# Two expert stages rewritten: 64 experts taken in pairs with matmul parts side by side, 8 experts' results written apart, deeper rings

## The reference

```
# layers 0, 2 (and a shared expert beside them); CAPACITY 160
h = einsum('ech,efh->ecf', buf, expert_w1)         # buf: 64 x 160 x 128
x1, x2 = split(h, 2, axis=-1)                      # 384 columns each
out = einsum('ecf,ehf->ech', x1 * silu(x2), expert_w2)
combined = zeros((T, H)).at[st].add(y)             # y = out * its gate
# layers 9, 11; capacity 1280
h = gelu(einsum('ecd,edf->ecf', padded_x, w1))     # 8 x 1280 x 128, 256 columns
out_w = out_rep * w_topk;  result = out_w.reshape(T, 2, D).sum(axis=1)
```

## Time and profile before

| | us |
|---|---|
| median of 3 runs (lowest, highest) | 4105.83 (4065.69, 4126.18) |
| the profiled execution | 4105.43 |
| its span, first to last instruction | 4103.7 |
| stretch of l0f1e, l0f2e | 262, 272 |
| stretch of l3f1e, l3f2e | 167, 164 |
| stretch of l2a, l3f1a, l3f2a | 404, 359, 367 |

### The profile page before, as it was taken

One profiled execution on the slowest core, in us unless ns is written; L12 is line 12 of the kernel. 1 busy time (PEld: TensorE's weight loads), 2 busy tenths in 40 slices (PEclk: granted clock), 3 DMA queues, 4 the chain that ended last, 5 costly groups with the idle time before them and its releaser, 6 DMA issues. The chain is left out here.

```text
span 4103.7 us, 70296 instructions
## 1 busy us (share of the span) xinstructions
PE 2727.5 (66%) x24900; PEld 1763.1 (43%) x24900; DVE 2230.5 (54%) x5930; ACT 1408.5 (34%) x2942; POOL 2017.8 (49%) x2409
## 2 busy tenths in 40 slices
PE   3348837544885546599966997361688876998361
PEld 1238824322774233355544554350233333554351
DVE  6743357567223524577734774214599995774313
ACT  1112213221111314156531664122666750664121
POOL 4757730174565302167731112686678772111685
...
GB/s 307 40 42 216 209 85 34 28 61 4 185 199 172 206 144 30 9 16 17 14 6 16 18 19 12 94 130 57 83 71 54 82 42 14 19 19 5 74 149 81
...
## 3 DMA queue, kind: packets, MB, share of 16 engines
...
...
## 5 line engine op out<-in xcount | busy, mean ns | idle before, releaser
L3256 PE MATMUL l3am_y<-l3am_hc,ident 128*128 128x512 f32 x512 | 285.6, 642 | 92.8 <-DVE l3am_hc L3165 92.7
L2945 POOL TENSOR_TENSOR l3am_db<-l3am_du,l3am_bs 128x512 f32<-128x512 f32 x256 | 317.8, 1271 | 43.9 <-DVE l3am_hh L3157 43.9
L3157 DVE TENSOR_TENSOR_SCAN l3am_hh<-l3am_dA,l3am_db 128x512 f32<-128x512 f32 x256 | 300.9, 1210 | 49.5 <-ACT l3am_dA L3065 48.3
L768 POOL TENSOR_TENSOR l2a_pT<-l2a_pT,l2a_kept 128x512 int32<-128x512 int32 x192 | 241.7, 1273 | 136.5 <-ACT l2a_pT L979 135.8
L2355 POOL DMA_INDIRECT l0f_table<-l0f2e_y,l0f2e_idx x128 | 178.8, 1397 | 133.6 <-DVE l0f2e_idx L2335 66.2
L869 DVE CUSTOM_DVE_ANT_0 l2a_junk<-l2a_s,l2a_addend 128x256 f32<-128x256 f32 x512 | 187.4, 421 | 83.0 <-PE l2a_s L1093 69.4
L2355 POOL DMA_INDIRECT l0f_table<-l0f1e_y,l0f1e_idx x128 | 178.8, 1397 | 80.7 <-issue 32.6
L2002 POOL DMA_INDIRECT l0f_rows<-l0f1r_row,l0f1r_idx x160 | 174.0, 1087 | 89.4 <-issue 86.6
L862 DVE TENSOR_REDUCE l3f2a_mx<-l3f2a_s 128x2 f32<-128x512 f32 x256 | 165.6, 686 | 67.2 <-PE l3f2a_s L1093 66.0
L862 DVE TENSOR_REDUCE l3f1a_mx<-l3f1a_s 128x2 f32<-128x512 f32 x256 | 165.6, 686 | 67.1 <-PE l3f1a_s L1093 65.8
L3256 PEld LDWEIGHTS l3am_y<-l3am_hc,ident 128*128 128x128 f32 x512 | 93.2, 198 | 227.1 <-DVE l3am_hc L3165 173.1
...
## 6 DMA issues: line engine op xcount, KB each, us to landing
...
l3f_rows<-blank SPq DMA_DIRECT2D x8, 1370.0 KB, 10.4
```

The lines of the kernel that those rows point to most:

```text
L768: self.nc.gpsimd.tensor_tensor(t, t, self.kept[:, f // 8 % 2, :].unsqueeze(1).to_broadcast([P, 2, 2 * P]), ALU.mult).then_inc(self.cut_g, 1)
L2945: G.tensor_tensor(db[j][n % 2][:, :], du[j][k % 2][:, :], bs[s // QUARTER][:, s % QUARTER, :], ALU.mult).then_inc(db_ready[j], 1)
L3157: V.tensor_tensor_scan(hh[j][n % 2][:, :], dA[j][n % 2][:, :], db[j][n % 2][:, :], 0.0, ALU.mult, ALU.add).then_inc(h_ready, 1)
L3256: T.matmul(yb[j][:, :], c.ident[:, :], hc[j][n % 2][:, :], start=(s == 0), stop=(s == N - 1)).then_inc(summed, 1)
```

## The change

1. **64 experts** (`paired_experts`): a unit is two experts, 320 slots, in pieces of 128, 128 and 64 rows; 32 units. `h` has one pair of banks for each expert q of the pair, used again by the next pair. In `output` the middle piece holds 32 rows of the first expert and 32 + 64 of the second, as three matmuls placed at columns 0, 32 and 64 of the array. DVE makes y with five operations. POOL issues three adds for a pair, each with waits for adds of the pair before; piece 0 goes to table 0, pieces 1 (but for its 32 first rows) and 2 to table 1. y is four deep.
2. **Matrices** (`Matrices`): a ring of 8 experts' matrices, the first 8 loaded during `route`. For 8 experts that is all of them.
3. **8 experts** (`experts`): a token's first choice goes to table 0, its second to table 1, by a number that `route` puts in the row, so the transfer writes and doesn't add; y and indices are five deep. A row is 144 numbers for 137; an empty slot's number is out of bounds and is skipped.
4. **Attentions**: strip 0 is filled by DVE, the others by POOL after `va`; `l3f1a` and `l3f2a` begin with the statistics before the weights are waited for; the mask of `l2a` is built in `l1at` (the last phase of `l1a`), its 16-fold compare and reduce replaced by 16 operations on 256 elements; in `l2a` ACT's normalisation moves from u = 1 to u = 4, behind the queries and keys.

The diff, cut to what is spoken of:

```diff
+            nc.vector.memset(c.blank[8][:, :, D + 8:], FAR).then_inc(blank_made, 1)
...
+    def strips(self, eng, n, made):
+        eng.memset(self.qk[n][:, :, 0, :], 0.0).then_inc(made, 1)
+        eng.memset(self.qk[n][:, :, 1, :], 1.0).then_inc(made, 1)
     def pool_setup(self, g):
         nc = self.nc
-        nc.gpsimd.memset(self.none[:, :], 0.0).then_inc(self.made, 1)
-        for t in self.qk:
-            nc.gpsimd.memset(t[:, :, 0, :], 0.0).then_inc(self.made, 1)
-            nc.gpsimd.memset(t[:, :, 1, :], 1.0).then_inc(self.made, 1)
...
+        for n in range(1, 4):
+            self.strips(nc.gpsimd, n, self.made)
+    def dve_setup(self):
+        self.nc.vector.memset(self.none[:, :], 0.0).then_inc(self.first_made, 1)
+        self.strips(self.nc.vector, 0, self.first_made)
...
-    def dve(self, v, finish, more=None):
+    def dve(self, v, finish, more=None, early=None):
         self.dve_stats(v, 0)
+        self.dve_setup()
+        if early:
+            early()
...
-            if u == 1 and self.real(b + 4) and self.kept is not None:
-                self.act_normal(a, b + 4)
...
+            if u == (1 if b == -4 else 4) and self.real(b + 4) and self.kept is not None:
+                self.act_normal(a, b + 4)
...
+        link(nc.vector.tensor_scalar(hit_k, cpos, gf[:, 0:1], None, ALU.is_equal))
+        for n in range(1, self.NG):
+            link(nc.vector.scalar_tensor_tensor(hit_k, cpos, gf[:, n:n + 1], hit_k, ALU.is_equal, ALU.max))
...
-                link(nc.vector.tensor_tensor(hit[:, :, :], cpos[:, :].unsqueeze(1).to_broadcast([P, NG, SEQ]),
-                                             gf[:, :].unsqueeze(2).to_broadcast([P, NG, SEQ]), ALU.is_equal))
-                link(nc.vector.tensor_reduce(hit_k[:, :], hit[:, :, :].rearrange("p g s -> p s g"), AX_X, ALU.max))
...
-        self.E, self.R = E, D + E + 1
+        self.E, self.R = E, D + (2 * E if self.apart else E + 1)
         self.rows = nc.dram_tensor(f"{name}_rows", (SLOTS, self.R), F32, kind="Internal").ap()
-        self.tables = [nc.dram_tensor(f"{name}_table{i}", (TOKENS + DUMPS * SUB, D), F32, kind="Internal").ap()
-                       for i in range(TABLES)]
+        self.all_tables = nc.dram_tensor(f"{name}_tables", (TABLES * TABLE, D), F32, kind="Internal").ap()
+        self.tables = [self.all_tables[i * TABLE:(i + 1) * TABLE, :] for i in range(TABLES)]
...
+            mats.load_first(sp)
...
+                if apart:
+                    second = hot[:, :, :].rearrange("p (t j) e -> p t j e", t=TPG)[:, :, 1, :]
+                    nc.vector.scalar_tensor_tensor(row[u][:, :, D + E:R], second, float(TABLE),
+                                                   token.to_broadcast([P, TPG, E]), ALU.mult, ALU.add).then_inc(steps, 1)
+                else:
+                    nc.vector.tensor_copy(row[u][:, :, R - 1:R], token).then_inc(steps, 1)
...
+class Matrices:
+    def __init__(self, ph, w1, w2, C1, KC, places):
...
+    def load(self, sp, e, place):
+        sp.dma_start(self.t1[place][:, :], self.w1[bass.ds(e, 1), :, :].rearrange("a p f -> (a p) f")
+                     ).then_inc(self.loaded[place], 16)
+        sp.dma_start(self.t2[place][:, :, :], self.w2[bass.ds(e, 1), :, :, :].rearrange("a p c d -> (a p) c d")
+                     ).then_inc(self.loaded[place], 16)
+    def load_first(self, sp):
+        for e in range(self.places):
+            self.load(sp, e, e)
+    LOADED = 32
...
-                if not isinstance(n, int) or n >= 2:
-                    v.wait_ge(added[p], 16 * A * ((U // 2) * i + u // 2))
-                v.wait_ge(loaded[u % U], 48 * use(i, u))
-                nc.vector.tensor_copy(idx[p][:, :], row[u % U][:, :, R - 1]).then_inc(idx_ready, 1)
+                if n >= RING:
+                    v.wait_ge(added[u % RING], 16 * A * (n // RING))
+                v.wait_ge(loaded[u % U], 16 * use(n))
+                nc.vector.tensor_copy(idx[u % RING][:, :], row[u % U][:, :, D + E + n // PER]).then_inc(idx_ready, 1)
                 v.wait_ge(o_done, n + 1)
-                nc.vector.tensor_tensor(y[p][:, :, :], ob[p][0:sub, 0:A * D].rearrange("p (a d) -> p a d", a=A),
-                                        row[u % U][:, :, bass.ds(D + expert(i, u), 1)].to_broadcast([sub, A, D]),
+                nc.vector.tensor_tensor(y[u % RING][:, :, :], ob[p][0:sub, 0:A * D].rearrange("p (a d) -> p a d", a=A),
+                                        row[u % U][:, :, bass.ds(D + n // PER, 1)].to_broadcast([sub, A, D]),
                                         ALU.mult).then_inc(y_ready, 1)
...
+                    g.indirect_dma_start(out=m.all_tables, out_offset=bass.IndirectOffsetOnAxis(
+                        ap=idx[u % RING][:, a:a + 1], axis=0), in_=y[u % RING][:, a, :], in_offset=None,
+                        bounds_check=last_row, oob_is_err=False).then_inc(added[u % RING], 16)
...
+def paired_experts(nc, c, name, m, mats, E, CAP, C1, KC):
...
+        U, RING, PIECES = 4, 4, (P, P, 64)
...
+        hb = [[ph.bank(f"h{q}{j}") for j in range(2)] for q in range(2)]
+        ob = [ph.bank(f"o{i}") for i in range(2)]
...
+        @block.tensor
+        def _(pe):
+            def turn(i, u, n):
+                pe.wait_ge(loaded[u], 32 * (i + 1))
+                if not first(n):
+                    pe.wait_ge(xe_ready, n)
+                for a, k in enumerate(PIECES):
+                    mm = nc.tensor.transpose(xb[:, a * P:a * P + k], row[u][0:k, a, 0:D], c.ident[0:k, 0:k])
+                mm.then_inc(turned, 1)
+            def hidden(i, u, n):
+                pe.wait_ge(xe_ready, n + 1)
+                for q in range(2):
+                    e = 2 * u + q
+                    pe.wait_ge(mats.loaded[e], mats.LOADED * (i + 1))
+                    if not first(n):
+                        pe.wait_ge(g_ready, 2 * n + q - 1)
+                    for f in range(C1):
+                        mm = nc.tensor.matmul(hb[q][f // 3][:, (f % 3) * S:(f % 3 + 1) * S],
+                                              mats.t1[e][:, f * P:(f + 1) * P], xeT[u % 2][:, q * S:(q + 1) * S],
+                                              start=True, stop=True)
+                    mm.then_inc(h_done, 1)
+            def output(i, u, n):
+                p = u % 2
+                pe.wait_ge(g_ready, 2 * n + 2)
+                if not isinstance(n, int) or n >= 2:
+                    pe.wait_ge(y_ready, n - 1)
+                def part(f, q, start, length, piece, place):
+                    return nc.tensor.matmul(ob[p][place:place + length, piece * D:(piece + 1) * D],
+                                            gT[p][q][:, f * S + start:f * S + start + length], mats.t2[2 * u + q][:, f, :],
+                                            start=(f == 0), stop=(f == KC - 1), tile_position=(0, place),
+                                            skip_group_check=True)
+                for f in range(KC):
+                    part(f, 0, 0, P, 0, 0)
+                for f in range(KC):
+                    part(f, 0, P, SHARED, 1, 0)
+                    part(f, 1, 0, 32, 1, 32)
+                    part(f, 1, 32, 64, 1, 64)
+                for f in range(KC):
+                    mm = part(f, 1, 96, 64, 2, 0)
+                mm.then_inc(o_done, 1)
...
+            def step(at):
+                i, u, n = at(0)
+                for q in range(2):
+                    a_.wait_ge(h_done, 2 * n + q + 1)
+                    if not first(n):
+                        a_.wait_ge(g_ready, 2 * n + q - 1)
+                    nc.scalar.activation(sT[q][:, :], hb[q][1][:, 0:F], ACT.Silu).then_inc(s_ready, 1)
...
             def step(at):
                 i, u, n = at(0)
                 p = u % 2
+                for q in range(2):
+                    v.wait_ge(s_ready, 2 * n + q + 1)
+                    nc.vector.tensor_tensor(gT[p][q][:, :], hb[q][0][:, 0:F], sT[q][:, :], ALU.mult).then_inc(g_ready, 1)
+                if not isinstance(n, int) or n >= RING:
+                    for t in added:
+                        v.wait_ge(t, 16 * (n - RING + 1))
+                v.wait_ge(loaded[u], 32 * (i + 1))
+                r, d = row[u], idx[u]
+                nc.vector.tensor_tensor(d[:, 0:2], r[:, 0:2, R - 1], table[:, :], ALU.add)
+                nc.vector.tensor_scalar(d[0:64, 2:3], r[0:64, 2, R - 1:R], float(TABLE), None, ALU.add).then_inc(idx_ready, 1)
+                v.wait_ge(o_done, n + 1)
+                for a, b, piece, q in ((0, P, 0, 0), (0, SHARED, 1, 0), (SHARED, 64, 1, 1), (64, P, 1, 1), (0, 64, 2, 1)):
+                    mm = nc.vector.tensor_scalar(y[u][a:b, piece, :], ob[p][a:b, piece * D:(piece + 1) * D],
+                                                 r[a:b, piece, bass.ds(D + 2 * n + q, 1)], None, ALU.mult)
+                mm.then_inc(y_ready, 1)
...
+            def step(at):
+                i, u, n = at(0)
                 hold(g, c.mark_g, idx_ready, n + 1)
```

(32 more changed lines are left out.)

294 lines of the change are left out of this document (200 added, 94 removed).

## The result

The changed kernel takes 4187.35 us (median of 4 runs, 4176.4 to 4210.17), the kernel before 4091.13 beside it (4 runs, 4065.69 to 4126.18): ratio 1.0236, 95% interval 1.0141 to 1.0332. Measured again in a later set it was 1.0233 (1.0181 to 1.0284). The forecast was 4084, 21 less than the kernel before in its profiled execution; measured by the medians are 96 more. The range, 3990 to 4175, was missed by 12 us, on the side of rival E, which had a chance of 0.06. The profiled execution has a span of 4179.4 us, 75.7 more than before.

The account below looks back on a forecast made before the run. 64-expert phases were taken as bound by the load's length through the ring, 8-expert phases by POOL. 4105.4 us + 110 (64 experts) - 96 (8 experts) - 35 (attentions) = 4084, range 3990 to 4175.

Parts of the forecast that it names:

- rival E: 64-expert phases: PE's idle time lowers the granted clock, at 0.72 a round of 12.2 us, 4254 us in all; chance 0.06.
- the round taken at whole clock: 64-expert phases: hidden, turn, output and PE's stop sum to 9.4 us a pair; both mixtures +110 us.
- E's own number: 64-expert phases: a clock of 0.72, giving a round of 12.2 us, +170 us and 4254 us in all.
- E's stated point of decision: 64-expert phases: total over 4188 us from a round of 11.1 us, a clock of 0.81.
- the step named as least trusted: 64-expert phases: y's five DVE operations at about 0.255 us each, 1.28 us in PE's stop.
- The chain PE, DVE, PE: 64-expert phases: `hidden` waits for gating products, queued on DVE behind y, which waits for `output`; PE stops 2.36 us a pair.
- Rival C: 64-expert phases: PE's stop doesn't bind, round 7.05 us, 147 us less, 3937 us in all; chance 0.04.
- The change of shape: Middle piece of `output`: each change between 32-row and 64-row parts costs 0.09 us, six changes a pair.
- What bounded before: 64-expert phases before the change: the load's length goes round through the ring, 7.43 and 8.00 us for two units.
- The 8 experts: 8-expert phases: transfers write in 0.97 us, 1.27 apart, POOL still first; -49 and -47, sum -96 us.
- The attentions: `l2a` mask built in `l1at`, -18 us; `l3f1a` and `l3f2a` statistics and fills, -8 each; sum -35 us.
- F: 64-expert phases: POOL's chain of landings binds past 7.6 us and costs over 2% from 9.2; chance 0.03.

Follow-up runs that it names:

- e12: Changed kernel plus four unneeded 128x128 matmuls behind each `output`, in PE's stop; 4107.29 us, ratio 1.002 to the kernel before.
- e2: Changed kernel plus eight unneeded 128x128 matmuls behind each `output`, in PE's stop; 4089.34 us, ratio 0.9986 to the kernel before.
- e3: Changed kernel with y made by two operations instead of five, gates laid in a column during `output`; 4040.1 us, ratio 0.9869 to the kernel before.
- e1: Changed kernel with DVE's gating products of pair n+1 put ahead of y of pair n; 3948.69 us, ratio 0.9673 to the kernel before.
- e5: Changed kernel with the middle piece's part of 64 rows made as two of 32; 4289.0 us on a slower chip, ratio 1.0211 to the kernel before.
- e7: Changed kernel with the 64-expert code of before, its ring 8 deep instead of 4; 4131.97 us on the slower chip, ratio 0.9828 to the kernel before.
- e9: Changed kernel as it is, run again in the third set; 4194.16 us, ratio 1.0233 to the kernel before.
- e4: Changed kernel with the 64-expert code of before put back, ring of 4; 3956.33 us, ratio 0.966 to the kernel before.
- e11: Changed kernel with gating products ahead of y and the middle piece in four parts of 32 rows; 3956.36 us, ratio 0.9674 to the kernel before.

## Why the prediction failed

**The step that failed is the dismissal of rival E**, the clock, and with it the round taken at whole clock: "a busy share of 7 in 9.4 lies above that" of a row at full clock, and so 0.06. The runs show the clock at 0.85 and rounds of 11.17 and 11.02 us for 9.83 at whole clock; e12 and e2 leave DVE's order as it is and have 1.00 and 9.83. I judged by the busy share of long stretches. The changed kernel has a higher share (156 us in 200) than the row of 2700 to 2750 (30 in 50) and loses the clock all the same.

Nor is it the length of one stop by itself. In that very stretch the weight loads once stand 2.81 us, longer than in the changed kernel, and what follows runs at whole clock, 8 loads in 0.97 us (the clock was 1.00 over all 50 us):

```profile
2706.56 0.97 PEld L2282 LDWEIGHTS l3f1e_o<-l3f1e_w,l3f1e_gT 128*128 128x128 f32 x8 [2.81 <-issue]
```

What e2, e3 and e12 show is that in this loop a stop of 1.64 us or less never took the clock. Which property of the stop or of the work around it decides, and why two rounds of three, stays open.

E's own number was too dark: the clock was 0.85, not 0.72, and by E's sign, "PEclk at 0.8 or below", it would have been ruled out. The round of 11.1 is just E's stated point of decision, which it gave to a clock of 0.81, since it started from 9.4 and not from 9.83.

**By terms.** From the first to the last y both mixtures take 202 us more than before, for 98 forecast. The difference of 104 is 78 by the clock (31 x 1.34 + 31 x 1.19, means of 11.17 and 11.02 against 9.83) and 25 by the round at whole clock (62 x 0.41). Of this 0.41, y has 0.32 (1.60 for 1.28, the step named as least trusted) and `turn` 0.17 (0.65 for 0.48); `hidden` was 0.09 shorter than taken, and `output` was 3.25 as taken. The rest of the 221, 19 us, lies ahead of the first y and behind the last, where 12 were taken. Without the 78 of the clock the kernel would have taken 4109, inside the range.

**The chain PE, DVE, PE** was right in kind and nearly in size: the stop 2.7 us for 2.36, and moving DVE's products takes it all away (e1). Rival C's round without a stop, 7.05, is 7.3 in e1.

**The change of shape** costs 0.12 to 0.14, taken as 0.09; that `output` came to 3.25 as taken is luck in part, since the overlap of the last part of 64 with the last piece was not in the sum. The Trainium skill, "TensorEngine Tiling (Array Packing)", section "Tiling Modes", says that changing the tiling mode drains TensorE. The traces agree: within the middle piece every row of the changed kernel with another shape starts 0.34 to 0.36 behind the last, and in e5, with one shape, these gaps are gone.

**What bounded before** was named too simply. The load was one of two: in e7 the load is no wait any more, the waits of DVE for the landings of the adds stay, and the pace is the same, on another chip. The forecast did not rest on it, since it laid the new loop beside the old pace.

**The 8 experts** came out as forecast (-99 for -96), with PE's 2.4 a unit indeed under POOL's 2.56. **The attentions** gave 45 for 35 in this profile, and that is partly luck. All thirteen profiles behind the change have the same attention code, and the three phases together are 18 to 46 us shorter in them than in the one profile before, 34 on the mean. `l2a` alone goes from -23 to -2, with the clock that was granted: 0.91 in the changed kernel's profile, 0.88 in e9, the same kernel, with -13, and 0.85 in e7 and e12 with -2 (kernel before: 0.89 over the same work). At nearly the clock of before, `l2a` (e5, e9) is 13 shorter, `l3f1a` (after, e1, e9) 6.5 to 7, `l3f2a` (e2, e4, e5) 7, together 26 for 35. The clock over these phases was no term of the sum. The edits in them were not tried apart.

**F** had its place in order: landings of 4.9 us at the median, 7.0 at most (2.9 at least), under 7.6, so they hold up nobody in the changed kernel, and PE waits behind them only when it is quicker, in e11.
